# TensorE's first expert of each layer turns its rows piece by piece, and hints take the place of visits to the expert bodies

## The reference

```python
def _L0_ffn_ref(inputs, gate_weight, wi, wo):      # E = 8 experts, C = 320 rows each
    logits = tokens @ gate_weight.T
    top1 = jnp.argmax(logits, axis=-1)
    ranks = jnp.cumsum(one_hot(top1, E), axis=0) - 1          # rows past C are dropped
    dispatch = jnp.einsum('tec,th->ech', sec_mask, tokens)
    hmid = jax.nn.gelu(jnp.einsum('ech,ehi->eci', dispatch, wi), approximate=False)
    eout = jnp.einsum('eci,eih->ech', hmid, wo)
    return jnp.einsum('tec,ech->th', combine_weights, eout)

x = L0_attn_x
x = x + 0.5 * _L0_ffn_ref(_layernorm(x), gate_weight, wi, wo)
x = x + _L0_attn_ref(_layernorm(x), Wu, bu, Wv, bv, Wg1, bg1, Wg2, bg2, conv_w, conv_b)
x = x + 0.5 * _L0_ffn_ref(_layernorm(x), gate_weight, wi, wo)
```

## Time and profile before

| | |
|---|---|
| three runs | 1083.21, 1087.63, 1088.45 us (median 1087.63) |
| profiled execution | 1083.39 us, span 1081.6 us |
| TensorE busy | 1028.1 us, 95% of the span |
| VectorE, ScalarE, GpSimd busy | 748.4, 543.5, 136.4 us |
| mean granted TensorE clock | 0.983 |
| chain that ended last | PE 84%, DVE 6%, issue 3%, ACT 3%, DMA 2% |
| fetches of TensorE's instructions (q8) | 28, 0.46 MB |

### The profile page before, as it was taken

One profiled execution on the slowest core, in us unless ns is written; L12 is line 12 of the kernel. 1 busy time (PEld: TensorE's weight loads), 2 busy tenths in 40 slices (PEclk: granted clock), 3 DMA queues, 4 the chain that ended last, 5 costly groups with the idle time before them and its releaser, 6 DMA issues.

```text
span 1081.6 us, 20118 instructions
## 1 busy us (share of the span) xinstructions
PE 1028.1 (95%) x7380; PEld 962.9 (89%) x7380; DVE 748.4 (69%) x1174; ACT 543.5 (50%) x851; POOL 136.4 (13%) x142
## 2 busy tenths in 40 slices
PE   9699999999999999699999996999999999999995
PEld 6599999999999999578787775999999999999995
DVE  8566566767677777478777675557778788765652
ACT  5445464665556565155233324455656756644441
POOL 3201111112020210100000013002012021120101
PEclk9899999999999999899999998999999999999998
DMA  8388546576455752310010035436476775764410
GB/s 313 116 297 292 207 143 222 172 240 225 167 207 195 248 168 89 113 68 1 1 39 27 29 143 178 155 134 225 167 266 218 235 247 178 258 217 148 148 39 25
DMA packets 83278, 177.34 MB, mean 164 GB/s; under 512 B 4192, under 2 KB 4704, under 8 KB 83168
## 3 DMA queue, kind: packets, MB, share of 16 engines
q1 hardware_dynamic: 75488, 152.61, 40.8%
q0 software_dynamic: 7168, 23.07, 6.2%
q10 hardware_dynamic: 576, 1.05, 0.3%
HBM read 162.04 MB, written 18.87 MB: 167 GB/s over the span
## 4 chain that ended last, share of the span: by engine, by line
PE 84%; DVE 6%; issue 3%; ACT 3%; DMA 2%; POOL 1%; DVEq 0%; POOLq 0%; ACTq 0%; SPq 0%
PE psH L1253 13%; PE acc L1265 13%; PE psH L1254 13%; PE psH L1255 13%; PE acc L1266 11%; PE acc L1261 9%; PE acc L1253 3%; PE acc L1255 3%; PE acc L1254 3%; DVE dtl L805 1%; DVE row_stats L838 1%; PE psH L1492 1%; PE psT L1589 1%; ACT eoT L689 1%; PE psT L1317 1%
## 5 line engine op out<-in xcount | busy, mean ns | idle before, releaser
L1253 PE MATMUL psH<-dth,wih 128*128 128x240 f32 (+5 forms) x1024 | 295.4, 289 | 1.3 <-issue 1.1
L1255 PE MATMUL psH<-dth,wil 128*128 128x240 f32 (+5 forms) x1024 | 293.3, 286 | 0.0
L1254 PE MATMUL psH<-dtl,wih 128*128 128x240 f32 (+5 forms) x1024 | 293.3, 286 | 0.0
L1266 PE MATMUL acc<-ht,wol 128*128 128x240 f32 (+5 forms) x1024 | 286.1, 279 | 0.0
L805 DVE TENSOR_TENSOR wol<-raw_wo,woh 128x1024 fp32r<-128x1024 f32 x128 | 155.6, 1222 | 107.2 <-ACT woh L622 106.6
L1265 PE MATMUL acc<-ht,woh 128*128 128x320 f32 (+3 forms) x1024 | 210.4, 299 | 0.0
L656 ACT ACTIVATE gel<-psH 128x320 f32<-128x320 f32 x256 | 112.1, 438 | 188.6 <-PE psH L1255 183.5
L622 ACT ACTIVATE woh<-raw_wo 128x1024 fp32r<-128x1024 f32 x128 | 134.6, 1059 | 123.0 <-PE acc L1266 122.9
L1253 PEld LDWEIGHTS psH<-dth,wih 128*128 128x128 f32 x1024 | 193.4, 189 | 2.9 <-issue 1.3
L1266 PEld LDWEIGHTS acc<-ht,wol 128*128 128x128 f32 x1024 | 193.6, 189 | 0.0
L1255 PEld LDWEIGHTS psH<-dth,wil 128*128 128x128 f32 x1024 | 193.5, 189 | 0.0
(11 more groups left out here) (200 smaller groups left out, 1172.1 us busy)
## 6 DMA issues: line engine op xcount, KB each, us to landing
raw_wi<-in_wi SPq DMA_DIRECT2D x64, 1024.0 KB
raw_wo<-in_wo SPq DMA_DIRECT2D x64, 1024.0 KB, 5.4
out_x<-xt SPq DMA_DIRECT2D x4, 1024.0 KB, 5.8
xt<-in_x SPq DMA_DIRECT2D x6, 512.0 KB, 8.4
xt<-x SPq DMA_DIRECT2D x3, 1024.0 KB, 9.7
raw_u<-in_wuT SPq DMA_DIRECT2D x1, 1024.0 KB
raw_u<-in_wvT SPq DMA_DIRECT2D x1, 1024.0 KB
xt<-in_x ACTq DMA_DIRECT2D x2, 256.0 KB, 3.9
```

The lines of the kernel that those rows point to most:

```text
L1253: pe.matmul(out, lh, rh, start=first, stop=False)
L1254: pe.matmul(out, lh, rl, start=False, stop=False)
L1255: return pe.matmul(out, ll, rh, start=False, stop=last)
L1266: return pe.matmul(bank[:, 0:w], ll, both[:, 0, 0:w], start=False, stop=False, skip_group_check=True)
```

## The change

Three edits, all in TensorE's program.

1. The loop's first iteration (`e` = 0) takes a path of its own: `turn_first` waits for each piece of `dn` and turns its four column blocks at once, raising `tokT_done` with those of the last piece; it waits for no `eoT` and leaves `turn_out` away. All iterations test `e` for this (`br_lt(e, 1)`). The first path always turns three pieces.
2. The visits go. Six hints stand in each layer, and they belong to the very branches of `dispatch` by which the later iterations go to the bodies. In layer 0 they stand after `ranks`, after `take_counts`, on both sides of `warm(WARM_LANES)`, and two at the end; in layer 1 four stand where `peek` stood in the mixer and two at the end.
3. Every body of both layers fills a block: `addr_align` ahead of its jump to `join` puts this jump in the last slot. A branch leads over the padding.

```diff
-                def peek(n=n):
-
-                    done = visits[n]
-                    if done:
-                        w = PLACED[len(done) - 1]
-                        done[-1] = nc.cur_bb
-                        pe.br(f"visit_{w}_{n}").branch_hint(marks.pop())
-                        nc.switch_bb(f"visited_{w}_{n}", parent=done[-1])
-                    if len(done) < VISITED[n]:
-                        done.append(None)
-                        marks.append(pe.mark_branch_hint_location())
+                def hint(n=n):
+
+                    hinted[n].append(pe.mark_branch_hint_location())
...
                 ranks(1)
+                if n == 0:
+                    hint()
                 take_counts()
+                if n == 0:
+                    hint()
                 tabulate(LT * n, SPLIT[n])
                 if n == 0:
+                    hint()
                     warm(WARM_LANES)
+                    hint()
                 tabulate(SPLIT[n], TILES)
-                for _ in range(3):
-                    peek()
+                for _ in range(2):
+                    hint()
...
+                def turn_first(s=s):
+
+                    for k in range(CHUNKS):
+                        pe.wait_ge(s.dn_done, k + 1)
+                        q = k * P
+                        for c in range(DC):
+                            ins = pe.transpose(TURNED[c][:, q:q + P], dn[:, k, c * P:(c + 1) * P], ident[:, :])
+                            if k == CHUNKS - 1:
+                                ins.then_inc(s.tokT_done, 1)
...
+                            if what != "first":
+                                ins.branch_hint(hinted[n][PLACED.index(w)])
...
-                    pe.br_lt(width, NARROW, on_true=f"narrow_{n}", on_false=f"wide_{n}")
+                    pe.br_lt(e, 1, on_true=f"first_{n}", on_false=f"later_{n}")
+                    with nc.body(f"first_{n}", parent=head, valid_engines=[pe.engine]):
+                        turn_first()
+                        dispatch("first", range(NW))
+                    with nc.body(f"later_{n}", parent=head, valid_engines=[pe.engine]):
+                        pe.br_lt(width, NARROW, on_true=f"narrow_{n}", on_false=f"wide_{n}")
...
                     with nc.body(f"run_{w}_{n}", parent=head, valid_engines=[pe.engine]):
                         expert(e, w)
+                        pe.addr_align(BLOCK, offset=BLOCK - 1, max_nops=0)
                         pe.br(f"join_{n}")
-                    if k >= VISITED[n]:
-                        continue
-                    with nc.body(f"visit_{w}_{n}", parent=visits[n][k], valid_engines=[pe.engine]):
-                        pe.addr_align(BLOCK, offset=BLOCK - 1, max_nops=0)
-                        pe.br(f"visited_{w}_{n}")
...
-                        peek(1)
+                        hint(1)
```

More of the change, by code:

```diff
@@ L51 @@
 HALF_B = (12, 14)
-VISITED = (2, 6)
 MOST = 12
@@ L1279, in _ @@
             width = pe.alloc_register("width")
-            visits = [[], []]
-            marks = []
+            hinted = [[], []]
             pe.wait_ge(pool_const, 1)
@@ L1522, in dispatch @@
                             if k < ks[-1]:
-                                pe.br_lt(width, k + 1, on_true=f"run_{w}_{n}", on_false=f"{what}_test_{k + 1}_{n}")
-                            else:
-                                pe.br(f"run_{w}_{n}")
+                                ins = pe.br_lt(width, k + 1, on_true=f"run_{w}_{n}",
+                                               on_false=f"{what}_test_{k + 1}_{n}")
+                            else:
+                                ins = pe.br(f"run_{w}_{n}")
+                            if what != "first":
+                                ins.branch_hint(hinted[n][PLACED.index(w)])
                 pe.wait_ge(s.taken_done, 1)
@@ L1545, in _ @@
                 over_bb = nc.cur_bb
-                for k, w in enumerate(PLACED):
+                for w in PLACED:
                     with nc.body(f"run_{w}_{n}", parent=head, valid_engines=[pe.engine]):
                         expert(e, w)
+                        pe.addr_align(BLOCK, offset=BLOCK - 1, max_nops=0)
                         pe.br(f"join_{n}")
-                    if k >= VISITED[n]:
-                        continue
-                    with nc.body(f"visit_{w}_{n}", parent=visits[n][k], valid_engines=[pe.engine]):
-                        pe.addr_align(BLOCK, offset=BLOCK - 1, max_nops=0)
-                        pe.br(f"visited_{w}_{n}")
                 nc.switch_bb(f"done_{n}", parent=over_bb)
```

## The result

The changed kernel takes 1111.98 us (median of four executions, 1108.73 to 1117.2), the kernel before 1088.0 beside it (1083.21 to 1088.45). The ratio is 1.0235, with a 95% interval of 1.0185 to 1.0285: 24.0 us slower by the medians, where I had forecast 1.1 us faster and had left no more than 0.07 for slower by over 0.5%. The profiled execution took 1111.01 us, its span is 1109.3 us against 1081.6.

What follows compares the result with a forecast made beforehand. TensorE, busy for 95% of the span, was taken as the bound. Gains of 0.7, 1.65 and 1.1 us less 2.35 us of slow clock made 1.1 us faster; it named 1085.5 us, range 1080.5 to 1090.

Steps and rivals of the forecast that it cites:

- The step that failed: Hints ahead of both layers' loops: two close together were assumed both to fetch, so jumps to bodies would find their code.
- rival (b): Jumps to 288, 320 and 272: paired hints lose their second; all three cost 5.1 us, 4.0 slower in sum; chance 0.18.
- a lone hint works: Layer 1's mixer, kernel before: the hint at 636.4 had a fetch, and the visit at 640.5 took 0.40 us, not 3.
- The price of a lost hint: Jumps to bodies: 1.4 us for 288, about 1.5 for 320 in layer 1, 2.2 for 272 in layer 0's third expert.
- The second failed step: Bodies in both layers' loops: each possible miss was priced once, with no repeat at later uses.
- Rival (d): Jumps to bodies: hints fetch nothing, blocks push one another out; 240 or 192 miss too, 3 us each; 1090 to 1094; chance 0.06.
- The visits of layer 0: Ahead of layer 0's first expert: two visits of 3.02 and 3.30 us let the sequencer reach `dn`'s wait just ahead of its last piece.
- the clearing at 41.66: Layer 0's first expert: banks cleared 1.92 us behind ScalarE's start at 39.74, instead of at 42.81.
- the first product at 42.6: Layer 0's first expert: first product starts at about 42.6 instead of 43.28, a gain of 0.7 us.
- the clock's rise at 44.5: Layer 0's first products: half speed until 44.5, losing 0.95 us; with layer 1, 2.35 us lost.
- The stall of 1.09 us: Layer 0's first product: TensorE's issue wait as body 288 crosses blocks; its own block, fetched ahead, gains 1.1 us.
- rival (c): The 14 boundaries between experts: added branches use up the sequencer's lead; at full price 5.9 us slower, 1093.5; chance 0.04.

Runs made afterwards that it cites:

- e12: Changed kernel with two adjacent hints a layer in place of six (layer 0: 288, then 304; layer 1: 304, then 320): 1103.94 us, ratio 1.0154.
- e8: Changed kernel with one hint a layer in place of six, last ahead of the loop (288 in layer 0, 320 in layer 1): 1098.79 us, ratio 1.0129.
- e15: Changed kernel with hints spaced apart: 272, then 288 in layer 0; 240, 192, then 320 in layer 1: 1096.68 us, ratio 1.0106.
- e4: Changed kernel without its twelve hints, all else the same: 1105.13 us, ratio 1.0172.
- e2: Kernel before, visits kept, with every body in its own block and its jump to join in the last slot: 1096.06 us, ratio 1.0099.
- e10: Kernel before with one visit in layer 0 (body 192) in place of two: 1093.65 us, ratio 1.0055.
- e11: Kernel before with one hint for 288, last ahead of the loop, in place of layer 0's two visits: 1096.07 us, ratio 1.0087.
- e9: Changed kernel with six visits a layer in place of hints, each into the body's own block, the jump back right behind the body: 1107.23 us, ratio 1.0177.
- e7: Kernel before without layer 0's two visits, its bodies laid end to end: 1094.67 us, ratio 1.009.
- e3: Changed kernel with the jump to join right behind the body's work, ahead of the padding: 1111.38 us, ratio 1.0246.
- e13: Kernel before with six idle warming products ahead of each visit of layer 0: 1085.88 us against 1085.67, ratio 1.0005.
- e5: Changed kernel with six visits a layer in place of hints, which by a flawed edit fetched empty blocks between bodies: 1158.29 us, ratio 1.0679.

## Why the prediction was wrong

**The step that failed** is this one: "Two hints within a few hundred ns have no row; I take it that both fetches are made." e12 shows that the second is lost, 320's at 0.1 us behind another. This is rival (b), and its premise "a lone hint works" is shown by e8., from which I had it, is a weaker ground than I thought: the fetch that I took for the hint's stands in the trace, but e8's and e15's hints that worked have no such row. By the changed kernel's order the second hints are those of 192, 288 and 320, and 288 and 320 are the bodies that the two layers start with.

**The price of a lost hint was mis-sized.** I put 288 and 320 at 1.4 and 1.5 us, from visits of 2.7 to 3.3 us and the work that would cover them. The jumps took 5.2 and 5.4 us, and the stands were 4.76 and 4.96.

**The second failed step was one I hardly wrote down:** that a body once fetched stays. I priced each body once. 272 is missed at its first use (156 us) and at its last (403), 320 at each of its three. Rival (d) named it in its brackets, "blocks push one another out", at 0.06 and 3 us a body, 1090 to 1094; it got neither the repeats nor the clock behind a stand, 2.6 and 2.3 us behind two of the five in mid-loop. Misses that return come without hints too (e4), with the visits of only two bodies in own blocks (e2), and in the unpadded layer 0 once one of its two visits is gone (e10, e11). Six visits keep 320 in (e9, e2). Why a visit keeps more than a hint or a miss does is open, and so is a rival that no run tests: nearly every edit also moved the code behind it, and none moved code and did nothing else.

**The visits of layer 0 were worth far more than two bodies.** I read them as 3.0 and 3.3 us of a sequencer that had time. With them and the blocks of 240 and 192 gone, e7 loses 0.9%, of which 2.9 us stand ahead of layer 1: through the block behind, they had brought in 288 and 272, which they don't name. The change took the packing away as well, which had 272 and the start of 288 share a block. With own blocks and these visits, e2 loses 1.0%.

**The rule of the Trainium skill** that I set aside ("Runtime: NRT & Kernel Launch", section "Instruction fetch mechanics") holds that a taken branch out of the current window of two pages forces a fetch. In the kernel before it doesn't: not one jump to a body misses in layer 0. But the misses of 3.3 to 5.4 us agree with its direction, and to take every jump over blocks as a possible fetch would have served me better than the sixteen cheap jumps back to the loop's own block. Those said nothing of jumps to six different bodies, and I argued from them.

**The other terms came out.** e8 tests them, since both first jumps are short there. In layer 0 I had the clearing at 41.66, the first product at 42.6 and the clock's rise at 44.5. e8 (last piece, clearing, first product):

```profile
38.31 0.81 ACT L638 ACTIVATE dn<-rows,facts_now 128x512 f32<-128x512 f32 x1 [1.21 <-DMA rows<-in_x,src_now]
...
41.50 0.27 PE L1448 MATMUL acc<-nil,ones 128*128 128x2 bf16 x4 [1.21 <-DVE dtl L804]
...
42.33 0.59 PE L1252 MATMUL psH<-dth,wih 128*128 128x288 f32 x1
```

```profile
41.50:45.80 4.30, 4.30 (x22) 4.19 (x23) 1.57 (x2) 1.71 (x3) 1.03 (x2) 0.50 0.84 306
```

The last piece was ready at 39.12, the clearing came 2.38 us behind it for the 2.56 forecast, and the clock stayed at 0.50 for 4.3 us behind the clearing, for 2.8 forecast. The stall of 1.09 us on 288's second block is gone, as forecast. In layer 1 of e8 the clearing at 680.22 came 2.53 us behind the last piece (677.69), and 4.65 before: 2.1 us gained for the 2.1 forecast. The clock rose 3.9 us behind that clearing, for 3.7 forecast. In no list of waits does an issue wait stand at the turns of a later expert, so rival (c) stays out. The terms were sound and small; they rested on a condition that was worth ten times as much.

The loss of 2.35% by parts, as far as the runs part it: twelve hints in a crowd cost 0.6% against none (changed kernel against e4; e3, which has the hints and ran beside e4, took 1111.38 us for its 1105.13). The two first bodies missed cost 0.4% by the ratios of e4 and e8, 6.3 us between their medians; in their traces the first clearing comes 4.3 us sooner in layer 0, and 4.4 in layer 1 counted from the load of the codes. The other 1.3% is what e8 still loses: 272, 240 and 320 missed in mid-loop, which the visits had held, and the low clock behind these stands. The runs are of different chips, and the intervals are 0.2% wide and more, so this is a rough account.

No version beat the kernel before. The nearest is e13, which is the same to within 0.25%.

## What to carry to other kernels

A sum of parts of a microsecond that rests on "the code is there" has to price that condition first. Count the blocks that a loop jumps among, and take from the trace not whether a jump to the loop's own block is cheap but whether each target, at each use, is. Before removing an early jump that seems to serve one target, look at what lies behind that target, since the next block comes with it. And if hints are used, one at a time, the one that matters right ahead of its use.

## What was new of the hardware

- A prefetch hint takes 31 to 50 ns of the sequencer. Alone, it cut jumps of 5.9 and 5.4 us to 0.46 and 0.32 us (e8). Of two hints 0.1 us apart the second had no effect (e12); 4.7 us behind another one a hint worked (e15). No fetch on q8 is recorded for the hints that worked in e8, while in the kernel before one stands behind the hint at 636.4; what makes the difference is open.
- A jump that misses takes 3.3 to 4.2 us in mid-loop (e5's aside; 240 in layer 1 took 1.5 to 2.0 in several runs), and 4.8 to 5.9 us ahead of a layer's first expert, where the DMA engines are busy with weights and rows; the cause of that difference wasn't tried.
- A block that is entered has the block behind it fetched: 304 was never missed behind 288 (0.34 us in e4, which has no hint or visit), and visiting 192 alone made 288 short (0.34 us, e10).
- With six bodies of one block each and the loop's own code, bodies are pushed out between two uses, and twelve hints make it worse (seven misses for five). Six visits in a row push out the code that they jump back to (4.88 us, e9).
- Behind a stand of TensorE in mid-loop the granted clock falls at times. In the changed kernel it was 0.50 for 6.8 us behind the stands of 3.3 and 3.6 us, and 1.00 behind those of 2.6, 2.7 and 2.9. Over the runs the length doesn't decide: in e8 a stand of 2.5 us was followed by 0.50 from 155.0 to 158.4, in e3 one of 3.2 us (at 156) was followed by 1.00. What does, I don't know.
